# Cross-attention on one core: the score products of gU with ctxT_lo, on 64 rows and two heads at a time

## The chip, the core and the metric

The kernel runs on one core of a Trainium2 chip. The time is the device time of the whole program in microseconds (us). Before the change the median of 3 runs is 317.23 us (317.16 to 317.6).

## The reference

```python
Q = (img_embed @ Wq).reshape(B, -1, H, D).transpose(0, 2, 1, 3)
K = (sent_embed @ Wk).reshape(B, -1, H, D).transpose(0, 2, 1, 3)
V = (sent_embed @ Wv).reshape(B, -1, H, D).transpose(0, 2, 1, 3)
score = jnp.einsum('bhqd,bhkd->bhqk', Q, K) / math.sqrt(D)
mask = (atten_mask != 0)[:, None, None, :]
score = jnp.where(mask, score, -jnp.inf)
attn = jax.nn.softmax(score, axis=-1)
ctx = jnp.einsum('bhqk,bhkd->bqhd', attn, V).reshape(B, -1, H * D)
out = ctx @ Wo + img_embed
mu = jnp.mean(out, axis=-1, keepdims=True)
var = jnp.var(out, axis=-1, keepdims=True)
return (out - mu) * jax.lax.rsqrt(var + EPS) * gamma + beta
```

`img_embed` is x (8 x 256 x 256), `sent_embed` is ctx_768 (8 x 256 x 192): a batch of 8, 256 queries and 256 keys, 8 heads of size 256. All is float32.

## The kernel before

**What is multiplied.** The weights are folded first. A = Wq Wk^T of a head is 256 x 192, so a head's scores are (x A) ctx^T, and C = Wv Wo of a head is 192 x 256. The query side of a head, g = A^T x^T, has 192 rows: 128 lower ones (gL) and 64 upper ones (gU).

**Split operands.** A float32 operand is cut into a high part, rounded to the type fp32r, and the low part that is left; a product is then high x high, high x low and low x high, each a matmul in fp32r that adds into the same place of a PSUM bank. For the 64 upper rows one tile `gU` holds both parts of a head one above the other: for head 0 of a pair the high part stands on partitions 0 to 63 and the low part on 64 to 127, for head 1 the other way round. The host lays the upper 64 rows of ctx^T twice, so `ctxT_hi[:, 1]` and `ctxT_lo[:, 1]` carry them on both halves of the partitions. A matmul of `gU` with `ctxT_hi[:, 1]` on 128 rows therefore gives high x high and low x high at once. One with `ctxT_lo[:, 1]` gives high x low and, beside it, low x low, which the split does not need.

**Steps.** The work is 32 steps, one for each batch and pair of heads (`STEPS`, `PAIRS`). There is no scheduler: each engine's queue is written out by hand, with semaphores between the engines, and 24 of the steps stand in a loop over the batches. In one step TensorE (PE) does `scores(t)` (20 matmuls: 2 heads, 2 halves of the queries, 5 products), `query_products(t + 1)` (18 matmuls into gU_bank and gL_bank), `output_products(t - 4)` (18) and `context_products(t - 3)` (20 into tL_bank and tU_bank). The first four steps also have `fold_C`, which makes C: line 359 on whole tiles, line 365 with 64 columns of the stationary operand, so that its outputs are 64 partitions high. Line 365 is the only place where a matmul uses less than 128 rows and 128 columns of the array.

**Around the scores.** `gU` and `gL_hi` are written by ScalarE (ACT, line 576), the low parts by VectorE (DVE, line 745), one step ahead of their use. DVE reads the score banks (`maxima`, line 797): head 0 after the first count of `scores_done`, head 1 after the second. Then come the exponentials (ACT, line 619), the division by the sums (GpSimd, POOL, line 1021), and a transposition through a scratch in DRAM.

**scores (line 388).** For each head and each query half it issues five matmuls of 128 x 128 by 256 into one half of the head's bank: gU x ctxT_hi, gU x ctxT_lo, gL_hi x ctxT_hi, gL_hi x ctxT_lo and gL_lo x ctxT_hi. All go through `split_products` (line 320), so that the profile gives them line 325.

Of the kernel before, what the change touches and what calls it, by code (L numbers as in the profile page):

```python
# [13 lines left out]
P = 128  # L14
# [10 lines left out]
UP = DL - P  # L25
PAIRS = H // 2
STEPS = B * PAIRS
QT = S // P
# [15 lines left out]
def attention_kernel(nc, xT, x, ctxT, ctx, mask, wqT, wkT, wvT, wo, gamma, beta, out, scratch):  # L44
    es = ExitStack()
    with es:
        def sb(name, shape, dt=F32):
            return es.enter_context(nc.sbuf_tensor(name, shape, dt))

        def bank(name, shape):  # L50
            return es.enter_context(nc.psum_tensor(name, shape, F32))

        def sem(name):
            return es.enter_context(nc.semaphore(name))
# [20 lines left out]
        gL_hi = sb("gL_hi", [P, 2, S + APART], F32R)[:, :, 0:S]  # L75
        gL_lo = sb("gL_lo", [P, 2, S + APART], F32R)[:, :, 0:S]
        gU = sb("gU", [P, 2, S + APART], F32R)[:, :, 0:S]
# [4 lines left out]
        ctxT_hi = sb("ctxT_hi", [P, 2, KV], F32R)  # L82
        ctxT_lo = sb("ctxT_lo", [P, 2, KV], F32R)
# [37 lines left out]
        score_bank = [bank("score_bank0", [P, QT, KV]), bank("score_bank1", [P, QT, KV])]  # L121
# [57 lines left out]
        g_hi_done = sem("g_hi_done")  # L179
        g_split = sem("g_split")  # L180
        scores_done = sem("scores_done")
# [139 lines left out]
        def _(pe):  # L321
            def split_products(into, pairs, first=True, last=True, shared=False):

                for n, (stationary, moving) in enumerate(pairs):
                    ins = nc.tensor.matmul(into, stationary, moving, start=first and n == 0,  # L325
                                           stop=last and n == len(pairs) - 1, skip_group_check=shared)
                return ins
# [57 lines left out]
                tile(gL_bank[:, 0, :], col)  # L385
                tile(gL_bank[:, 1, :], col + P).then_inc(g_product, 1)

            def scores(t, j, b, heads=(0, 1)):

                if j == 0:  # L390

                    pe.wait_ge(ctxT_split, b + 1)
                for hh in heads:
                    if hh == 0:

                        pe.wait_ge(g_hi_done, 3 * t + 3)
                        pe.wait_ge(g_split, 3 * t + 2)
                    for q in range(QT):
                        rows = slice(q * P, (q + 1) * P)
                        hi, lo, up = gL_hi[:, hh, rows], gL_lo[:, hh, rows], gU[:, hh, rows]  # L400
                        split_products(score_bank[hh][:, q, :],
                                       [(up, ctxT_hi[:, 1, :]), (up, ctxT_lo[:, 1, :]),
                                        (hi, ctxT_hi[:, 0, :]), (hi, ctxT_lo[:, 0, :])], last=False)
                        if hh == 0 and q == 0:

                            pe.wait_ge(g_split, 3 * t + 3)
                        ins = split_products(score_bank[hh][:, q, :], [(lo, ctxT_hi[:, 0, :])], first=False)
                    ins.then_inc(scores_done, 1)

            def transposes(t):  # L410

# [107 lines left out]
            def step(t, j, b, folds=()):  # L519

                jb, bb = (j - LAG) % PAIRS, b - 1 if j < LAG else b
                ja, ba = (j + 1) % PAIRS, b + 1 if j == PAIRS - 1 else b
                scores(t, j, b)
                query_products(t + 1, ja, ba)
                if not (isinstance(t, int) and t < OUT_LAG):
                    output_products(t - OUT_LAG, j, b - 1)
                for pair in folds:
                    fold_C(pair)
                if not (isinstance(t, int) and t < LAG):
                    context_products(t - LAG, jb, bb)  # L530
# [15 lines left out]
            with pe.Fori(1, B - 1) as b:  # L546
# [3 lines left out]
                step(PAIRS * b + 5, 1, b + 1)  # L550
            step(STEPS - 2, 2, B - 1)
            scores(STEPS - 1, 3, B - 1)

            output_lowers(STEPS - 5, 3, B - 2)
# [587 lines left out]
```

## Time and profile before

| | |
|---|---|
| median of 3 runs | 317.23 us |
| profiled execution | 317.46 us |
| its span, first to last instruction | 315.7 us |
| PE busy | 308.8 us (98%) |
| PE's weight loads busy | 302.7 us (96%) |
| DVE, ACT, POOL busy | 253.1, 222.1, 181.4 us |
| mean granted TensorE clock | 0.997 |

PE is the row of the matmuls, PEld that of the weight loads, which run beside the matmuls. The matmuls are pipelined: a record lasts 0.28 us, while the next one starts about 0.11 us after it. So the time of a matmul in a dense stream is the distance from one start to the next. An fp32 matmul leaves two records, one in fp32r leaves one.

### The profile page before, as it was taken

The page shows a single profiled execution, that of the slowest core. Times are in us where ns is not written, and L with a number is a line of the kernel's source. Part 1 is how long each engine was busy: PE and PEld are TensorE (multiplying, and loading weights), DVE is VectorE, ACT ScalarE, POOL GpSimd, SP SyncE. Part 2 cuts the span into 40 slices and gives each one's busy share as a digit, 9 for nine tenths or more (in the row PEclk, how much of TensorE's full clock was granted, in tenths as well). Part 3 has the DMA queues.
Part 4 walks back from the last instruction along what each step waited for, and adds up shares of the span by engine and source line. Part 5 has one row for each costly group of instructions (what it writes and reads, how often), then busy time and mean ns, then how long its engine had stood idle before and what let it go on. Part 6 is the DMA issues. An engine that isn't in the chain of part 4 may idle for free.

```text
span 315.7 us, 8051 instructions
## 1 busy us (share of the span) xinstructions
PE 308.8 (98%) x2584; PEld 302.7 (96%) x2584; DVE 253.1 (80%) x721; ACT 222.1 (70%) x601; POOL 181.4 (57%) x183
## 2 busy tenths in 40 slices
PE   8999999999999999999999999999999999999993
PEld 7898889999999999999999999999999999999992
DVE  0467778777999879987998889987998889985686
ACT  2446678768867787678777797678767887777640
POOL 1123476457864587558855586458755686457212
PEclk9999999999999999999999999999999999999998
DMA  7995443464354553474445544364355535440101
GB/s 248 373 408 228 137 151 117 158 217 135 92 168 139 199 165 129 145 246 136 133 125 193 184 138 162 128 216 156 110 191 153 199 103 185 143 158 2 35 0 66
DMA packets 46912, 50.27 MB, mean 159 GB/s; under 512 B 3505, under 2 KB 37041, under 8 KB 46897
## 3 DMA queue, kind: packets, MB, share of 16 engines
q1 hardware_dynamic: 46608, 49.56, 46.7%
q10 hardware_dynamic: 288, 0.52, 0.7%
q8 instruction: 8, 0.13, 0.2%
q14 instruction: 8, 0.06, 0.1%
HBM read 32.24 MB, written 17.83 MB: 159 GB/s over the span
## 4 chain that ended last, share of the span: by engine, by line
PE 95%; DMA 2%; DVE 1%; SPq 1%; POOLq 0%; issue 0%; POOL 0%
PE score_bank L325 25%; PE out_bank L325 19%; PE gL_bank L325 14%; PE tL_bank L325 13%; PE tU_bank L325 9%; PE gU_bank L325 7%; DMA wq_raw<-in_wqT 2%; PE spare_bank L325 1%; PE spare_bank L359 1%; PE tL_bank L359 1%; PE tL_bank L341 1%; PE tU_bank L341 1%; PE tU_bank L365 1%; PE out_bank L365 1%; PE out_bank L341 0%; PE spare_bank L341 0%
## 5 line engine op out<-in xcount | busy, mean ns | idle before, releaser
L1021 POOL TENSOR_TENSOR probs<-probs,inv_sum 128x512 f32<-128x512 f32 x64 | 66.7, 1043 | 84.0 <-DVE inv_sum L808 83.4
L619 ACT ACTIVATE probs<-neg_scores,neg_max 128x256 f32<-128x256 f32 x128 | 64.2, 503 | 36.8 <-DVE neg_max L797 36.7
L1044 POOL TENSOR_TENSOR pT_lo<-pT_raw,pT_hi 128x512 fp32r<-128x512 f32 x60 | 76.7, 1298 | 8.6 <-ACT pT_hi L576 8.6
L797 DVE CUSTOM_DVE_ANT_0 neg_scores<-score_bank,mask_bias 128x256 f32<-128x256 f32 x128 | 49.2, 421 | 6.5 <-PE score_bank L325 4.0
L818 DVE STREAM_TRANSPOSE squares<-probs 128x512 f32<-128x512 f32 x60 | 42.4, 706 | 0.2
L576 ACT ACTIVATE tL_hi<-tL_bank 128x512 fp32r<-128x512 f32 x31 | 18.5, 598 | 28.4 <-PE tL_bank L325 28.4
L325 PE MATMUL score_bank<-ctxT_hi,gU 128*128 128x256 f32 x128 | 36.4, 284 | 0.0
L325 PE MATMUL score_bank<-ctxT_hi,gL_hi 128*128 128x256 f32 x128 | 36.0, 281 | 0.0
L325 PE MATMUL score_bank<-ctxT_lo,gU 128*128 128x256 f32 x128 | 35.9, 281 | 0.0
L325 PE MATMUL score_bank<-ctxT_hi,gL_lo 128*128 128x256 f32 x128 | 35.9, 280 | 0.0
L325 PE MATMUL score_bank<-ctxT_lo,gL_hi 128*128 128x256 f32 x128 | 35.8, 280 | 0.0
L325 PE MATMUL gL_bank<-xT_hi,A_lo 128*128 128x256 f32 x128 | 35.3, 276 | 0.0
L325 PE MATMUL gL_bank<-xT_lo,A_hi 128*128 128x256 f32 x128 | 35.3, 276 | 0.0
L325 PE MATMUL gL_bank<-xT_hi,A_hi 128*128 128x256 f32 x128 | 35.3, 276 | 0.0
L745 DVE TENSOR_TENSOR tL_lo<-tL_bank,tL_hi 128x512 fp32r<-128x512 f32 x31 | 21.4, 689 | 17.2 <-ACT tL_hi L576 17.1
L576 ACT ACTIVATE pT_hi<-pT_raw 128x512 fp32r<-128x512 f32 x60 | 34.3, 622 | 0.0
L325 PE MATMUL out_bank<-CL_lo,tL_hi 128*128 128x256 f32 x118 | 32.6, 276 | 0.0
L325 PE MATMUL out_bank<-CL_hi,tL_hi 128*128 128x256 f32 x118 | 32.6, 276 | 0.0
L325 PE MATMUL out_bank<-CL_hi,tL_lo 128*128 128x256 f32 x118 | 32.6, 276 | 0.0
L745 DVE TENSOR_TENSOR gU<-gU_bank,gU 64x256 fp32r<-64x256 f32 x64 | 27.1, 423 | 2.1
L845 DVE TENSOR_TENSOR tU<-tU_bank,tU_moved 64x256 f32<-64x256 f32 x62 | 26.0, 419 | 1.6 <-ACT tU_moved L660 0.6
L325 PEld LDWEIGHTS score_bank<-ctxT_hi,gU 128*128 128x128 f32 x128 | 24.0, 188 | 1.4 <-issue 1.2
(167 smaller groups left out, 980.6 us busy)
## 6 DMA issues: line engine op xcount, KB each, us to landing
scratch<-squares SPq DMA_DIRECT2D x30, 512.0 KB, 2.7
pT_raw<-scratch SPq DMA_DIRECT2D x120, 128.0 KB, 2.9
xT_raw<-in_xT SPq DMA_DIRECT2D x8, 256.0 KB, 4.4
ctxT_raw<-in_ctxT SPq DMA_DIRECT2D x8, 256.0 KB, 4.6
wo_raw<-in_wo SPq DMA_DIRECT2D x4, 512.0 KB, 13.7
x_res<-in_x SPq DMA_DIRECT2D x8, 256.0 KB, 3.0
out<-y_out SPq DMA_DIRECT2D x7, 256.0 KB, 2.5
wq_raw<-in_wqT SPq DMA_DIRECT2D x3, 512.0 KB, 7.6
```

The lines of the kernel that those rows point to most:

```text
L325: ins = nc.tensor.matmul(into, stationary, moving, start=first and n == 0, stop=last and n == len(pairs) - 1, skip_group_check=shared)
L341: ins = nc.tensor.matmul(dst[:, i * DL:(i + 1) * DL], wq_raw[:, h * DT + d, i * P:(i + 1) * P], wk_raw[:, h * DT + d, :], start=d == 0, st ...
L359: ins = nc.tensor.matmul(lower[:, hh, :], wv_raw[:, h * DT + d, 0:P], wo_raw[:, h * DT + d, :], start=d == 0, stop=d == DT - 1)
L365: ins = nc.tensor.matmul(upper[hh * UP:(hh + 1) * UP, 0, :], wv_raw[:, h * DT + d, P:DL], wo_raw[:, h * DT + d, :], start=d == 0, stop=d = ...
L576: return nc.scalar.activation(dst, src, ACT.Copy)
L619: nc.scalar.activation(probs[j % 2][:, n, :], neg_scores[:, n, :], ACT.Exp, bias=neg_max[:, n:n + 1], scale=-1.0, accum_out=row_sum[:, n:n ...
L745: return nc.vector.tensor_tensor(dst, whole, hi.bitcast(F32), ALU.subtract)
L797: nc.vector.tensor_tensor_reduce(out=neg_scores[:, n, :], in0=score_bank[hh][:, q, :], in1=mask_bias[:], scale=-SCALE, scalar=3.0e38, op0= ...
L818: nc.vector.transpose(squares[:, :, rows, :].rearrange("p s n c -> p n s c"), probs[j % 2][:, rows, :].rearrange("p n (s c) -> p n s c", c ...
L845: nc.vector.tensor_tensor(tU[part, :], places("tU", t)[0][part, hh, :], tU_moved[part, :], ALU.add).then_inc(tU_summed, 1)
L1021: nc.gpsimd.tensor_tensor(probs[j % 2][:, rows, :], probs[j % 2][:, rows, :], inv, ALU.mult) \
L1044: nc.gpsimd.tensor_tensor(pT_lo[j % 2][:, k].rearrange("p hh (q i r) -> p (hh q) i r", q=QT, i=ROWS), pT_raw[j % 2][:, k].rearrange("p i n ...
```

## The change

The product gU x ctxT_lo is computed on the 64 rows that hold the high part of a head alone: partitions 0 to 63 for head 0, 64 to 127 for head 1. The two heads' matmuls of a query half stand one behind the other (`pair_of_heads`), on different rows of the array and into different banks. One such pair stands ahead of query half 0 of head 0, and one ahead of query half 1 of head 0. The other four products of each head and half follow as before (`rest`). Since a pair writes both halves of both banks ahead of the rest, only the pair of query half 0 opens the accumulation of a bank. The waits at the head of a step stand for both heads; the wait for gL_lo stands ahead of the last product of head 0's first half, as before.

```diff
--- before.py
+++ after.py
@@ -385,27 +385,40 @@
                 tile(gL_bank[:, 0, :], col)
                 tile(gL_bank[:, 1, :], col + P).then_inc(g_product, 1)
 
-            def scores(t, j, b, heads=(0, 1)):
+            def scores(t, j, b):
 
                 if j == 0:
 
                     pe.wait_ge(ctxT_split, b + 1)
-                for hh in heads:
-                    if hh == 0:
-
-                        pe.wait_ge(g_hi_done, 3 * t + 3)
-                        pe.wait_ge(g_split, 3 * t + 2)
-                    for q in range(QT):
-                        rows = slice(q * P, (q + 1) * P)
-                        hi, lo, up = gL_hi[:, hh, rows], gL_lo[:, hh, rows], gU[:, hh, rows]
-                        split_products(score_bank[hh][:, q, :],
-                                       [(up, ctxT_hi[:, 1, :]), (up, ctxT_lo[:, 1, :]),
-                                        (hi, ctxT_hi[:, 0, :]), (hi, ctxT_lo[:, 0, :])], last=False)
-                        if hh == 0 and q == 0:
-
-                            pe.wait_ge(g_split, 3 * t + 3)
-                        ins = split_products(score_bank[hh][:, q, :], [(lo, ctxT_hi[:, 0, :])], first=False)
-                    ins.then_inc(scores_done, 1)
+                pe.wait_ge(g_hi_done, 3 * t + 3)
+                pe.wait_ge(g_split, 3 * t + 2)
+
+                def pair_of_heads(q):
+
+                    rows = slice(q * P, (q + 1) * P)
+                    for hh, part in enumerate((slice(0, UP), slice(UP, P))):
+                        split_products(score_bank[hh][:, q, :], [(gU[part, hh, rows], ctxT_lo[part, 1, :])],
+                                       first=q == 0, last=False, shared=True)
+
+                def rest(hh, q):
+
+                    rows = slice(q * P, (q + 1) * P)
+                    hi, lo, up = gL_hi[:, hh, rows], gL_lo[:, hh, rows], gU[:, hh, rows]
+                    split_products(score_bank[hh][:, q, :],
+                                   [(up, ctxT_hi[:, 1, :]), (hi, ctxT_hi[:, 0, :]), (hi, ctxT_lo[:, 0, :])],
+                                   first=False, last=False, shared=True)
+                    if hh == 0 and q == 0:
+
+                        pe.wait_ge(g_split, 3 * t + 3)
+                    return split_products(score_bank[hh][:, q, :], [(lo, ctxT_hi[:, 0, :])], first=False,
+                                          shared=True)
+
+                pair_of_heads(0)
+                rest(0, 0)
+                pair_of_heads(1)
+                rest(0, 1).then_inc(scores_done, 1)
+                rest(1, 0)
+                rest(1, 1).then_inc(scores_done, 1)
 
             def transposes(t):
```

The queue of PE in the second step, at head 0. A row is one matmul: bank written, moving operand, stationary operand, and the rows and columns of the output. Before:

```order
L325 MATMUL score_bank0<-ctxT_hi,gU 128x256
L325 MATMUL score_bank0<-ctxT_lo,gU 128x256
L325 MATMUL score_bank0<-ctxT_hi,gL_hi 128x256
L325 MATMUL score_bank0<-ctxT_lo,gL_hi 128x256
L325 MATMUL score_bank0<-ctxT_hi,gL_lo 128x256
L325 MATMUL score_bank0<-ctxT_hi,gU 128x256
L325 MATMUL score_bank0<-ctxT_lo,gU 128x256
L325 MATMUL score_bank0<-ctxT_hi,gL_hi 128x256
L325 MATMUL score_bank0<-ctxT_lo,gL_hi 128x256
L325 MATMUL score_bank0<-ctxT_hi,gL_lo 128x256
```

and at the same place now:

```order
L325 MATMUL score_bank0<-ctxT_lo,gU 128x256
L325 MATMUL score_bank1<-ctxT_lo,gU 128x256
L325 MATMUL score_bank0<-ctxT_hi,gU 128x256
L325 MATMUL score_bank0<-ctxT_hi,gL_hi 128x256
L325 MATMUL score_bank0<-ctxT_lo,gL_hi 128x256
L325 MATMUL score_bank0<-ctxT_hi,gL_lo 128x256
L325 MATMUL score_bank0<-ctxT_lo,gU 128x256
L325 MATMUL score_bank1<-ctxT_lo,gU 128x256
L325 MATMUL score_bank0<-ctxT_hi,gU 128x256
L325 MATMUL score_bank0<-ctxT_hi,gL_hi 128x256
L325 MATMUL score_bank0<-ctxT_lo,gL_hi 128x256
L325 MATMUL score_bank0<-ctxT_hi,gL_lo 128x256
```

The rows with ctxT_lo and gU are the ones on 64 rows, and each now has one of score_bank1 behind it; four matmuls on 128 rows stand between the two pairs. Behind that, at head 1, stood ten matmuls, and now eight:

```order
L325 MATMUL score_bank1<-ctxT_hi,gU 128x256
L325 MATMUL score_bank1<-ctxT_hi,gL_hi 128x256
L325 MATMUL score_bank1<-ctxT_lo,gL_hi 128x256
L325 MATMUL score_bank1<-ctxT_hi,gL_lo 128x256
L325 MATMUL score_bank1<-ctxT_hi,gU 128x256
L325 MATMUL score_bank1<-ctxT_hi,gL_hi 128x256
L325 MATMUL score_bank1<-ctxT_lo,gL_hi 128x256
L325 MATMUL score_bank1<-ctxT_hi,gL_lo 128x256
```

Head 1's two products with ctxT_lo and gU have gone from here to the pairs.

## Rows read from the trace of the kernel before

**Rows 1.** The page, busy times of the engines and their shares of the span

```profile
span 315.7 us, 8051 instructions
PE 308.8 (98%) x2584; PEld 302.7 (96%) x2584; DVE 253.1 (80%) x721; ACT 222.1 (70%) x601; POOL 181.4 (57%) x183
```

**Rows 2.** The page, the chain that ended last

```profile
PE 95%; DMA 2%; DVE 1%; SPq 1%; POOLq 0%; issue 0%; POOL 0%
```

**Rows 3.** Waits: who waited for whom, us in total, times, longest us

```profile
POOL probs L1021 <- DVE inv_sum L808: 83.4, 58, 4.4
ACT probs L619 <- DVE neg_max L797: 36.7, 56, 1.9
ACT tL_hi L576 <- PE tL_bank L325: 28.4, 30, 2.2
...
PE score_bank L534 <- POOL zeros L1006: 1.1, 1, 1.1
...
PE tL_bank L341 <- DMA wq_raw<-in_wqT: 0.5, 1, 0.5
```

**Rows 4.** Windows: busy us and count of each engine, clock, DMA share

```profile
50.00:304.00 254.00, 254.00 (x2219) 254.00 (x2218) 216.73 (x614) 191.81 (x516) 161.24 (x154) 1.00 0.45 146
```

**Rows 5.** Timeline of PE: start us, us, instruction; a step and the next

```profile
155.50 0.28 PE L325 MATMUL score_bank<-ctxT_hi,gU 128*128 128x256 f32 x1
155.62 0.28 PE L325 MATMUL score_bank<-ctxT_lo,gU 128*128 128x256 f32 x1
155.74 0.28 PE L325 MATMUL score_bank<-ctxT_hi,gL_hi 128*128 128x256 f32 x1
...
157.85 0.28 PE L325 MATMUL gU_bank<-xT_hi,A_hi 128*128 128x256 f32 x1
...
158.53 0.28 PE L325 MATMUL gL_bank<-xT_hi,A_hi 128*128 128x256 f32 x1
158.65 0.28 PE L325 MATMUL gL_bank<-xT_lo,A_hi 128*128 128x256 f32 x1
158.76 0.28 PE L325 MATMUL gL_bank<-xT_hi,A_lo 128*128 128x256 f32 x1
...
164.20 0.28 PE L325 MATMUL score_bank<-ctxT_hi,gU 128*128 128x256 f32 x1
```

**Rows 6.** Timeline of the weight loads at that step's start

```profile
155.50 0.19 PEld L325 LDWEIGHTS score_bank<-ctxT_lo,gU 128*128 128x128 f32 x1
155.62 0.19 PEld L325 LDWEIGHTS score_bank<-ctxT_hi,gL_hi 128*128 128x128 f32 x1
```

**Rows 7.** Timeline of PE around L365, from several windows

```profile
39.55 0.81 PE L359 MATMUL tL_bank<-wo_raw,wv_raw 128*128 128x256 f32 x3
39.98 0.38 PE L359 MATMUL tL_bank<-wo_raw,wv_raw 128*128 128x256 f32 x1
40.29 0.44 PE L365 MATMUL tU_bank<-wo_raw,wv_raw 128*64 128x256 f32 x2
40.55 0.61 PE L365 MATMUL tU_bank<-wo_raw,wv_raw 128*64 128x256 f32 x4
41.31 0.39 PE L325 MATMUL score_bank<-ctxT_hi,gU 128*128 128x256 f32 x1
41.53 0.28 PE L325 MATMUL score_bank<-ctxT_lo,gU 128*128 128x256 f32 x1
41.65 0.28 PE L325 MATMUL score_bank<-ctxT_hi,gL_hi 128*128 128x256 f32 x1
```

**Rows 8.** Timeline of the weight loads there, idle time before in brackets

```profile
40.28 0.15 PEld L365 LDWEIGHTS tU_bank<-wo_raw,wv_raw 128*64 128x64 f32 x2 [0.33 <-issue]
41.31 0.19 PEld L325 LDWEIGHTS score_bank<-ctxT_hi,gU 128*128 128x128 f32 x1 [0.39 <-issue]
41.41 0.19 PEld L325 LDWEIGHTS score_bank<-ctxT_lo,gU 128*128 128x128 f32 x1
```

**Rows 9.** Tiles tU_bank and score_bank: ns min/median/max, first and last start

```profile
L365 PEld LDWEIGHTS tU_bank<-wo_raw,wv_raw x16: 132/136/137, 33.0 to 40.8; 128*64 128x64 f32 x16
L365 PE MATMUL tU_bank<-wo_raw,wv_raw x16: 379/379/430, 33.0 to 41.0; 128*64 128x256 f32 x16
L325 PEld LDWEIGHTS score_bank<-ctxT_lo,gU x128: 187/188/192, 19.4 to 287.8; 128*128 128x128 f32 x128
```

**Rows 10.** Timeline of PE at its last step, behind a wait for DVE

```profile
308.03 0.39 PE L325 MATMUL spare_bank<-CL_hi,tL_hi 128*128 128x256 f32 x1
308.26 0.28 PE L325 MATMUL spare_bank<-CL_lo,tL_hi 128*128 128x256 f32 x1
```

**Rows 11.** Timeline of PE, from fp32r matmuls to fp32 ones

```profile
16.42 0.28 PE L325 MATMUL gL_bank<-xT_hi,A_lo 128*128 128x256 f32 x1
16.54 0.48 PE L341 MATMUL tL_bank<-wk_raw,wq_raw 128*128 128x192 f32 x2
```

**Rows 12.** Timeline of DVE around that step

```profile
153.75 0.69 DVE L745 TENSOR_TENSOR gL_lo<-gL_bank,gL_hi 128x512 fp32r<-128x512 f32 x1
159.49 0.42 DVE L797 CUSTOM_DVE_ANT_0 neg_scores<-score_bank,mask_bias 128x256 f32<-128x256 f32 x1
```

## Prediction

> **What bounds the kernel now.** I read the busy times first [rows 1]: PE has an instruction in flight for 308.8 of 315.7 us, and weight loads for 302.7 us; DVE follows with 253.1 us, ACT with 222.1, POOL with 181.4. The chain of work that ended last is PE for 95%, and a quarter of the span of it stands in score_bank [rows 2]. Then I asked who PE waits for [rows 3]: twice in the whole execution, 1.1 and 0.5 us, both before 10 us. In the loop it waits for nobody, and the clock is 1.00 between 50 and 304 us, which is the level of 2.4 GHz [rows 4]. So the kernel is a queue of matmuls on one engine. What is to be priced is how far apart two matmuls start, not how long one is drawn (0.28 us, since they are pipelined). In the timeline of a step [rows 5] the scores go from 155.50 to 157.85 us with 20 matmuls: 0.1175 us each. The gL_bank matmuls behind them start 0.113 apart. The step's loads start at the same distance, each just as the matmul ahead starts [rows 6]: a load is hidden behind the matmul ahead of it, and takes nearly as long. The next step starts at 164.20 us, 8.70 us later.
>
> **The change, part by part.** It touches PE alone. Each of the 32 steps had 20 score matmuls on 128 rows. It still has 20: 16 as before, and 4 on 64 rows, in two pairs. The two of a pair use different rows of the array and write different banks. So 32 x 2 = 64 pairs take the place of 128 full matmuls.
>
> *The gain by itself.* If the two of a pair run side by side, one slot of 0.118 us goes per pair. Side by side isn't seen for halves by rows before, but it is for halves by columns: L365 computes on 128 x 64 tiles, and its records come in twos [rows 7]. The first two take 0.44 us together where one takes 0.430 [rows 9], so the second starts some 0.013 us behind the first. The four from 40.55 on take 0.61 where one takes 0.379: the fourth starts 0.23 us behind the first, which is one more 0.013 and one step of 0.216 between the twos. (L359 has that step too, 0.215, but for single records: three take 0.81, one 0.379.) So a pair costs 0.118 + 0.013 = 0.131 in place of 2 x 0.1175 = 0.235 us: 0.104 us less, 64 x 0.104 = 6.7 us in all.
>
> *The switch.* The same place is the only one where PE changes from whole-array matmuls to part-array ones and back. Its cost can be read off as a whole. The last L359 matmul starts at 39.98 us, the second score matmul behind L365 at 41.53 us: 1.55 us. Between lie one L359 slot of 0.215 us (as above), four L365 steps of 0.216 and one score slot of 0.12: 1.20 us. The way in and out cost 0.355 us. The loads show what it is made of [rows 8]. The one of L365 isn't started with the matmul ahead, at 39.98, but at 40.28, and the first score load at 41.31, with no producer to wait for (both are put down to "issue"). The last two of L365 start at about 40.98 (40.55 and two steps) and would free the array at 41.20, so that load comes 0.11 late, and then stands in the open: second score matmul at 41.53, less a slot of 0.12, gives a true start at 41.41. That is 0.21 us out, hence 0.145 in. The way in is cheaper by its narrower load, 136 ns against 188 [rows 9]. The pairs of the change load 128 columns, so I put the way in at 0.145 + 0.052 = 0.197, the way out at 0.21: 0.41 us per visit.
>
> That an open load alone costs about half of that is seen where PE waited for DVE: load and matmul begin at 308.03, the next matmul 0.23 later, where 0.12 is usual [rows 10]. And it isn't the change between fp32 and fp32r operands: at 16.54 us fp32 matmuls of L341 follow fp32r ones of L325, all on whole tiles, at a plain 0.12 us [rows 11].
>
> The Trainium skill (TensorEngine Tiling (Array Packing), Key Properties) says that changing the tiling mode, and not just the tile, drains TensorE. The column halves agree with 0.355 us. By this rule row halves pay as well; what they pay no page says and no trace here shows.
>
> *Bounds of that unknown.* From below: halves by rows need no switch, and the pair's loads are hidden as all others are: 0 per visit. From above: a switch at 0.41 and the two loads or the two matmuls one behind the other, another 0.11: 0.52. I take 0.41 as the nearest row by kind, with the loads side by side as those of L365 are (two in 0.15 us, where one takes 0.136) [rows 8, 9].
>
> *The order of the work.* The kernel comes back to whole-array matmuls between the two pairs of a step, since half 0 of head 0 stands between: two visits a step, 64 in all, none shared. Every one is on the path, because PE waits for nobody.
>
> *Edits at nothing.* Bank 1 is written at the head of a step instead of ten matmuls later. Its readers, DVE's maxima of head 1, are through by 159.49 + 0.42 = 159.91 us, and the next step starts at 164.20 [rows 5, 12]. The wait for gL_lo stands ahead of the sixth score matmul instead of the fifth; it was written by 153.75 + 0.69 = 154.44 us, 1 us ahead of the step [rows 12]. Head 0 is complete after ten slots as before, head 1 after 18. Behind PE, ACT and POOL idle (POOL 83.4 us, ACT 36.7 and 28.4 [rows 3]); they neither lose by a slower PE nor hold up one that is 2% faster.
>
> *Sum.* Per pair 0.41 + 0.131 - 0.235 = +0.306 us; 64 x 0.306 = +19.6 us. The profiled execution took 317.46 us (a span of 315.7 and 1.8 around it), so 337.0 us. The median of the plain runs is 0.23 us below the profiled one: 336.8 us. Its own range is 333 (64 x 0.25, the visit at 0.355 us) to 338.
>
> **The rivals.**
> 1. *Row halves need no switch.* For it: all operands are fp32r, the outputs use all 128 partitions as before, only rows are left out, and L365 shows that parts of the array do run side by side. Against: nothing in the trace tells rows from columns, and columns pay. Price: -6.7 us, 310.5 us. This is the case on the other side; it decides below 0.104 us a visit. The Trainium skill (TensorE: Matmul & The Clock Gate, Part 3, The mechanism) speaks for it: loads are pulled ahead of running matmuls where the row groups differ, and matmuls of different tiles start about 4 ns apart. By its figure the gain would be an estimated 7.2 us, 310 us; L365 has 13 ns between its twos, by columns.
> 2. *No switch, but loads one at a time.* The change removes no load: 2584 loads before and after, each spaced 0.113 to 0.118 us. If loads of different rows can't overlap, the pair's two take two slots, and nothing is gained: 317.2 us. For it: the spacing is as much the loads' as the matmuls' [rows 6]. Against: L365's loads start 13 ns apart.
> 3. *Switch, and a pair one behind the other.* +0.306 + 0.11 = +0.41 us x 64 = +26.5 us: 343.7 us.
> 4. *A cheaper switch*, one way or without the open load: 0.15 to 0.3 a visit, +3 to +13 us: 320 to 330 us.
>
> **How the numbers follow.** A measurement of this kernel can tell about 0.2%, 0.6 us. Forecast 0.52; rival 1 0.22; rival 2 0.08; rival 3 0.12; rival 4 0.06. Slower: 0.52 + 0.12 + 0.06 = 0.70. Rival 2 lands within 0.2% for 0.06 and a little faster for 0.02; so faster 0.24, same 0.06. The range must reach from the forecast to rival 1, the larger of the others: 310 to 340 us, with rival 3 left out.
>
> **What would show it.** Right: the step's period grows from 8.70 to about 9.31 us; idle time of the weight loads ahead of `score_bank<-ctxT_lo,gU`, put down to issue, where it was 0.0; both score matmuls of a pair about 13 ns apart; the matmul behind a pair 0.3 us behind it; 2584 matmuls still. Wrong: a period of 8.49 us with the load of a pair standing beside the matmul ahead of it (rival 1), or 8.70 with loads of a pair 0.11 apart (rival 2), or a pair's matmuls over 0.1 us apart (rival 3).

## The result, and the profile after

The changed kernel takes 342.0 us (median of 4 runs, 341.87 to 342.15) against 317.33 us (4 runs) of the kernel before: a ratio of 1.0777, 95% interval 1.0758 to 1.0795. The forecast was 336.8 us with a range of 310 to 340. The direction is right, the time lies outside the range.

The page of the changed kernel, busy times. They answer to [rows 1]:

```profile
span 340.2 us, 8051 instructions
PE 332.4 (98%) x2584; PEld 309.6 (91%) x2584; DVE 254.3 (75%) x721; ACT 222.0 (65%) x601; POOL 180.8 (53%) x183
```

The span is 24.5 us longer, with the same number of matmuls. PE is as full as before, while the weight loads now have gaps. The wait list names no new wait of PE (its one wait for a weight transfer, before 10 us, is 1.4 us where it was 0.5 [rows 3], and its first L325 matmul starts at 14.32 us, before at 14.28); the other engines wait longer for it (POOL 108.8 us where it was 83.4 [rows 3]). So the time is in PE's own queue, at a clock of 1.00 as before (the windows below).

Two words are used from here on. A *slot* is the distance from one matmul's start to the next. A *visit* is PE going over to tiles of 64 rows and back to whole ones.

The start of a step in the timeline of PE (start us, us, instruction), to be read beside [rows 5]:

```profile
166.79 0.28 PE L325 MATMUL tU_bank<-pT_lo,ctxU 128*128 128x256 f32 x1
167.00 0.39 PE L325 MATMUL score_bank<-ctxT_lo,gU 64*128 64x256 f32 x2
167.31 0.39 PE L325 MATMUL score_bank<-ctxT_hi,gU 128*128 128x256 f32 x1
167.54 0.28 PE L325 MATMUL score_bank<-ctxT_hi,gL_hi 128*128 128x256 f32 x1
```

and the weight loads there:

```profile
166.68 0.19 PEld L325 LDWEIGHTS tU_bank<-pT_lo,ctxU 128*128 128x128 f32 x1
167.00 0.19 PEld L325 LDWEIGHTS score_bank<-ctxT_lo,gU 64*128 64x128 f32 x2
167.31 0.19 PEld L325 LDWEIGHTS score_bank<-ctxT_hi,gU 128*128 128x128 f32 x1
167.42 0.19 PEld L325 LDWEIGHTS score_bank<-ctxT_hi,gL_hi 128*128 128x128 f32 x1
```

This is the picture of L365 [rows 7, 8], now by rows. The two loads of a pair stand together, and so do its two matmuls: two in 0.39 us, where one takes 0.381:

```profile
L325 PE MATMUL score_bank<-ctxT_lo,gU x128: 380/381/383, 19.3 to 310.9; 64*128 64x256 f32 x128
```

They aren't started beside the matmul of 166.79 but 0.21 us behind it, and the load that follows comes at 167.31. From 166.79 to 167.54 pass 0.75 us, where four slots of 0.1175 (0.47) stood before: +0.28 us for a pair. 64 x 0.28 = 17.9 us.

That leaves 24.5 - 17.9 = 6.6 us. They are not at the pairs at all. (The visits of the first four steps are cheaper than the later ones; counted start by start over the whole trace, the visits take 17.6 us and the rest is 6.9.) The gL_bank matmuls, which the change doesn't touch, in the changed kernel:

```profile
170.90 0.28 PE L325 MATMUL gL_bank<-xT_hi,A_hi 128*128 128x256 f32 x1
171.02 0.28 PE L325 MATMUL gL_bank<-xT_lo,A_hi 128*128 128x256 f32 x1
171.14 0.28 PE L325 MATMUL gL_bank<-xT_hi,A_lo 128*128 128x256 f32 x1
171.25 0.28 PE L325 MATMUL gL_bank<-xT_hi,A_hi 128*128 128x256 f32 x1
```

They start 0.118 us apart, before 0.113 [rows 5]. The same holds for all 56 matmuls of a step that aren't scores. 56 x 0.0045 = 0.25 us a step, and with the two pairs (0.56) a step is 0.81 us longer. Windows, one row per kernel, from 60 to 280 us (busy us and count of each engine, granted clock, DMA share, GB/s), first the kernel before, then the changed one:

```profile
60.00:280.00 220.00, 220.00 (x1924) 220.00 (x1923) 191.79 (x548) 168.05 (x455) 143.56 (x137) 1.00 0.49 159
```

```profile
60.00:280.00 220.00, 220.00 (x1758) 207.65 (x1757) 174.75 (x496) 153.99 (x417) 132.46 (x126) 1.00 0.44 144
```

At 76 matmuls a step, 1924 are 8.69 us a step and 1758 are 9.51: 0.82 us longer, as the two parts give. The granted clock is 1.00 in both, its level of 2.4 GHz, so it has no part in this.

### The profile page after: what moved, and what is told of

It reads as the page before. It is cut to its first block, busy times and chain, and to the rows that moved or that the text cites. A ratio compares the mean times of both kernels' runs of the same rounds, so it can differ in the third digit from the quotient of the medians.

```text
span 340.2 us, 8051 instructions
## 1 busy us (share of the span) xinstructions
PE 332.4 (98%) x2584; PEld 309.6 (91%) x2584; DVE 254.3 (75%) x721; ACT 222.0 (65%) x601; POOL 180.8 (53%) x183
## 4 chain that ended last, share of the span: by engine, by line
PE 95%; DMA 2%; DVE 1%; SPq 0%; POOLq 0%; issue 0%; POOL 0%
PE score_bank L325 28%; PE out_bank L325 18%; PE gL_bank L325 13%; PE tL_bank L325 13%; PE tU_bank L325 9%; PE gU_bank L325 7%; DMA wq_raw<-in_wqT 2%; PE spare_bank L325 1%; PE tL_bank L359 1%; PE spare_bank L359 1%; PE tL_bank L341 1%; PE tU_bank L341 1%; PE out_bank L365 1%; PE tU_bank L365 1%; PE out_bank L341 0%; PE spare_bank L341 0%
## 5 line engine op out<-in xcount | busy, mean ns | idle before, releaser
L1034 POOL TENSOR_TENSOR probs<-probs,inv_sum 128x512 f32<-128x512 f32 x64 | 66.6, 1041 | 108.8 <-DVE inv_sum L821 108.8
L325 PE MATMUL score_bank<-ctxT_hi,gU 128*128 128x256 f32 x128 | 42.7, 334 | 0.0
L325 PE MATMUL score_bank<-ctxT_lo,gL_hi 128*128 128x256 f32 x128 | 36.3, 284 | 0.0
L325 PE MATMUL score_bank<-ctxT_hi,gL_hi 128*128 128x256 f32 x128 | 36.0, 282 | 0.0
L325 PE MATMUL score_bank<-ctxT_hi,gL_lo 128*128 128x256 f32 x128 | 36.0, 281 | 0.0
L325 PE MATMUL gL_bank<-xT_hi,A_lo 128*128 128x256 f32 x128 | 35.8, 280 | 0.0
L325 PE MATMUL gL_bank<-xT_hi,A_hi 128*128 128x256 f32 x128 | 35.7, 279 | 0.0
L325 PE MATMUL gL_bank<-xT_lo,A_hi 128*128 128x256 f32 x128 | 35.7, 279 | 0.0
L325 PE MATMUL out_bank<-CL_hi,tL_lo 128*128 128x256 f32 x118 | 33.0, 280 | 0.0
L325 PE MATMUL out_bank<-CL_lo,tL_hi 128*128 128x256 f32 x118 | 32.9, 279 | 0.0
L325 PE MATMUL out_bank<-CL_hi,tL_hi 128*128 128x256 f32 x118 | 32.9, 279 | 0.0
L325 PEld LDWEIGHTS score_bank<-ctxT_hi,gU 128*128 128x128 f32 x128 | 24.0, 187 | 8.2
L325 PE MATMUL tL_bank<-pT_hi,ctxL_hi 128*128 128x256 f32 x124 | 24.7, 280 | 0.0
```

The lines of the kernel that those rows point to most:

```text
L1034: nc.gpsimd.tensor_tensor(probs[j % 2][:, rows, :], probs[j % 2][:, rows, :], inv, ALU.mult) \
```

## The experiments

Below, the pace is the length of a slot among whole-tile matmuls: 0.113 us is the fast one, 0.118 the slow one. Three theories of the slow pace stand at the start. A: any restart of the stream of matmuls (a load that isn't hidden behind a matmul) sets it to 0.118 us, until something among the score matmuls brings back 0.113. B: only going over to part-array tiles does. C, later called O: the order of the score matmuls does. P came in after the first four runs: the places of the operands in SBUF have a part. In the edits `up`, `hi`, `lo` are gU, gL_hi and gL_lo.

**Order alone.** The pairs on all rows, at the changed kernel's places:

```diff
-                    for hh, part in enumerate((slice(0, UP), slice(UP, P))):
+                    for hh, part in enumerate((slice(0, P), slice(0, P))):
```

> The changed kernel's order of the score matmuls, but with gU x ctxT_lo on all 128 rows, as before the change. Theory A (going over to 64-row tiles and back costs about 0.39 us a visit, and each such restart also sets the stream of matmuls to a pace of 0.118 us in place of 0.113): no visit, no restart, so 317.3 us and 0.113 between gL_bank matmuls. Theory B (the switch itself, and nothing else that restarts PE, sets the slow pace): 317.3 us too. Theory C (the new order, two banks in turn and one start for a bank, sets the slow pace): 56 matmuls x 32 steps x 0.0045 us = 8 us more, 325 us.

Measured: 325.21 us (before 317.5; ratio 1.0236, 1.0219 to 1.0253). A and B miss it, C names it within 0.3 us. With no 64-row matmul in the kernel, gL_bank goes at 0.118:

```profile
153.47 0.28 PE L325 MATMUL gL_bank<-xT_hi,A_hi 128*128 128x256 f32 x1
153.59 0.28 PE L325 MATMUL gL_bank<-xT_lo,A_hi 128*128 128x256 f32 x1
153.71 0.28 PE L325 MATMUL gL_bank<-xT_hi,A_lo 128*128 128x256 f32 x1
```

The edit keeps three things of the new order together: the sequence of the products, the two banks in turn, and the single opening of a bank. No run separates them.

**Both pairs in front.**

```diff
                 pair_of_heads(0)
-                rest(0, 0)
                 pair_of_heads(1)
+                rest(0, 0)
```

> The changed kernel with both pairs at the head of the step, one behind the other: one visit a step in place of two. All theories: the visits fall from 64 to 32, and 32 x 0.39 = 12.5 us go: 329.5 us, if the pace stays at 0.118 us behind the scores. Theory A adds: 16 whole score matmuls now follow the restart without a second one (8 in the changed kernel), which is where the stream of the kernel before finds back to 0.113; if it does so here, another 7 to 8 us go: 322 us. Theory B: the pace stays slow, 329.5 us.

Measured: 329.12 us (1.0360, 1.0343 to 1.0377), with gL_bank at 0.118 still. That fits B and C, and not the quick recovery that A allowed. From the changed kernel it is 12.9 us down for 32 visits fewer, 0.40 us each. The one visit that is left, with its two pairs:

```profile
151.41 0.40 PE L325 MATMUL tU_bank<-pT_lo,ctxU 128*128 128x256 f32 x2
151.74 0.50 PE L325 MATMUL score_bank<-ctxT_lo,gU 64*128 64x256 f32 x4
152.17 0.39 PE L325 MATMUL score_bank<-ctxT_hi,gU 128*128 128x256 f32 x1
152.39 0.28 PE L325 MATMUL score_bank<-ctxT_hi,gL_hi 128*128 128x256 f32 x1
```

The second tU_bank matmul starts at 151.53 (0.40 for two, 0.28 for one). From there to 152.39 pass 0.86 us, where six slots of 0.118 (0.71) stood: +0.15 for a visit with two pairs against +0.28 with one. So a second pair in the same visit saves about 0.12 us.

**One 64-row matmul at the head of a step**, without a partner:

```diff
+                        part = slice(0, UP if hh == 0 and q == 0 else P)
                         split_products(score_bank[hh][:, q, :],
-                                       [(up, ctxT_hi[:, 1, :]), (up, ctxT_lo[:, 1, :]),
+                                       [(gU[part, hh, rows], ctxT_lo[part, 1, :]), (up, ctxT_hi[:, 1, :]),
```

> The kernel before with one matmul of each step, gU x ctxT_lo of head 0 and query half 0, on 64 rows and first in the step: one visit a step, with no partner beside it. Price of the visit alone: 32 x 0.39 = 12.5 us. Theory A: 19 whole score matmuls follow, the pace is back at 0.113 us before gL_bank: 330 us. Theory B: the switch leaves the pace at 0.118: 8 us more, 338 us.

Measured: 329.19 us (1.0365, 1.0348 to 1.0383): 11.7 us for 32 visits, 0.37 each, and no more. (In the loop alone a step takes 9.09 us where it took 8.70, 0.39 a visit; the first four are cheaper.) The timeline shows the passage, with the fourth group of score matmuls:

```profile
153.76 0.28 PE L325 MATMUL score_bank<-ctxT_hi,gL_lo 128*128 128x256 f32 x1
153.88 0.28 PE L325 MATMUL score_bank<-ctxT_lo,gU 128*128 128x256 f32 x1
153.99 0.28 PE L325 MATMUL score_bank<-ctxT_hi,gU 128*128 128x256 f32 x1
154.11 0.28 PE L325 MATMUL score_bank<-ctxT_hi,gL_hi 128*128 128x256 f32 x1
154.22 0.28 PE L325 MATMUL score_bank<-ctxT_lo,gL_hi 128*128 128x256 f32 x1
```

0.12 up to 153.88, 0.113 from there on, and so through the rest of the step. B, already missed by the first run, falls: this kernel goes over to a 64-row tile in every step, and the slow pace doesn't last.

**One 64-row matmul at the end of the scores:** gU x ctxT_lo moved to the end of each group of five, on 64 rows in the last.

> The kernel before with one matmul of each step, gU x ctxT_lo of head 1 and query half 1, on 64 rows and last among the step's scores: one visit a step. Theory A: the restart stands behind the score matmuls, nothing brings the pace back, the 56 others of a step go at 0.118 us: 317.3 + 12.5 + 8 = 338 us. Theory B: the same 338 us; if the place of the visit doesn't matter, this run and the one with the visit at the head are equal, under theory A this one is 8 us longer.

Measured: 337.80 us (1.0635, 1.0618 to 1.0653), as A and B both said. But the edit had moved the product in all four groups, and the pace was slow ahead of the visit too, so the order could explain it as well. The pair of runs with the last group alone, below, separates the two.

**A restart with no switch.** The kernel before, and behind the scores of each step:

```diff
+                pe.wait_ge(scores_done, 2 * t + 2)
```

> The kernel before, with one wait more in each step: behind its 20 score matmuls PE waits until the last of them is done (scores_done). All on whole tiles, order as before. Price of the wait itself, from a matmul's 0.28 us less its slot and an open load of 0.11: about 0.3 us, 32 x 0.3 = 9.6 us. Theory A (any restart of the stream sets the slow pace, 0.118 us, until score matmuls bring the fast one back): the 56 others of a step are slow, 8 us more, 335 us. Theory B (only going over to part-array tiles does it): 327 us. Theory O (the order of the score matmuls alone decides the pace, restarts don't): 327 us.

Measured: 334.76 us (two runs, 333.86 and 335.66; 1.0538, 1.0469 to 1.0606). The time is A's (the two runs are 0.5% apart); its parts are another matter. A step whose pace is slow behind the wait:

```profile
165.44 0.28 PE L325 MATMUL score_bank<-ctxT_lo,gL_hi 128*128 128x256 f32 x1
165.55 0.28 PE L325 MATMUL score_bank<-ctxT_hi,gL_lo 128*128 128x256 f32 x1
165.89 0.39 PE L325 MATMUL gU_bank<-xT_hi,A_hi 128*128 128x256 f32 x1
166.11 0.28 PE L325 MATMUL gU_bank<-xT_lo,A_hi 128*128 128x256 f32 x1
166.23 0.28 PE L325 MATMUL gU_bank<-xT_hi,A_lo 128*128 128x256 f32 x1
166.35 0.28 PE L325 MATMUL gU_bank<-xT_hi,A_hi 128*128 128x256 f32 x1
...
```

It was 0.113 up to 165.55 and is 0.118 from 166.11 on, on whole tiles throughout. But the step ahead of it, in the same trace, stays fast:

```profile
156.45 0.28 PE L325 MATMUL score_bank<-ctxT_hi,gL_lo 128*128 128x256 f32 x1
156.86 0.38 PE L325 MATMUL gU_bank<-xT_hi,A_hi 128*128 128x256 f32 x1
157.08 0.28 PE L325 MATMUL gU_bank<-xT_lo,A_hi 128*128 128x256 f32 x1
157.19 0.28 PE L325 MATMUL gU_bank<-xT_hi,A_lo 128*128 128x256 f32 x1
157.31 0.28 PE L325 MATMUL gU_bank<-xT_hi,A_hi 128*128 128x256 f32 x1
```

Of 26 restarts between 50 and 290 us, 20 left the slow pace and 6 the fast one, every fourth. It isn't chance. The 20 are alike (the next matmul starts 0.334 us behind the last score matmul), and so are the 6 (0.410 us), and the 6 are always the same step of a batch, that of the fourth pair of heads. There `query_products` goes on to the next batch: it reads the first columns of A, and PE has a further wait, for xT_split, right behind the added one. The fourth step ahead of the loop goes over to the same operands behind the same further wait (at 45.01 us), but starts after 0.334 us, and its gL_bank matmuls go at 0.118. So the operands alone don't make it fast; what goes with the pace in all of these restarts is how late the next matmul starts. So A needs a softer form: a restart can set either pace, and mostly sets the slow one. The wait itself was about as dear as expected: 165.55 to 166.11 is 0.56 us where two slots (0.23) stood, 0.33 us; 156.45 to 157.08 gives 0.40.

**The last group alone, on 64 and on 128 rows.** The first three groups as in the kernel before; in the fourth gU x ctxT_lo comes last, once on 64 rows and once on 128. The cut below is shortened, and `FROM` stands for `UP` in the first kernel and for `0` in the second:

```diff
+                        late = hh == 1 and q == 1
...
+                                             [(lo, ctxT_hi[:, 0, :])] + ([(gU[FROM:, hh, rows], ctxT_lo[FROM:, 1, :])] if late else []),
```

> The kernel before, with only the step's last group of five changed: for head 1 and query half 1, gU x ctxT_lo comes last and on 64 rows (the first 15 score matmuls of a step stay as they were). One visit a step, behind the scores. Theories A and B: fast pace at the group before, lost by the visit: 317.3 + 12.5 + 8 = 338 us. Theory O: if the same order on 128 rows keeps the fast pace, so does this one: 330 us.

> The same order as the kernel with the 64-row matmul last, but on 128 rows: no visit. Theories A and B: 317.3 us, as the first 15 score matmuls have brought the fast pace by then. Theory O: 317.3 us if the order of the first three groups decides, 325 us if that of the last.

Measured: 337.64 us on 64 rows (1.0628, 1.0598 to 1.0659), 317.55 us on 128 (1.0000, 0.9989 to 1.0011). This is the clean pair: one order, and going over to 64 rows costs 20.1 us. The 64-row kernel at the visit:

```profile
158.01 0.28 PE L325 MATMUL score_bank<-ctxT_lo,gL_hi 128*128 128x256 f32 x1
158.13 0.28 PE L325 MATMUL score_bank<-ctxT_hi,gL_lo 128*128 128x256 f32 x1
158.33 0.38 PE L325 MATMUL score_bank<-ctxT_lo,gU 64*128 64x256 f32 x1
158.64 0.39 PE L325 MATMUL gU_bank<-xT_hi,A_hi 128*128 128x256 f32 x1
158.87 0.28 PE L325 MATMUL gU_bank<-xT_lo,A_hi 128*128 128x256 f32 x1
158.99 0.28 PE L325 MATMUL gU_bank<-xT_hi,A_lo 128*128 128x256 f32 x1
159.11 0.28 PE L325 MATMUL gU_bank<-xT_hi,A_hi 128*128 128x256 f32 x1
```

0.113 ahead of it, 0.118 behind. From 158.13 to 158.87 pass 0.74 us where three slots of 0.113 (0.34) stood: 0.40 for the visit, 12.8 us for 32. The rest, 7.3 us, is the pace. O as the only cause falls.

**Placement.** The order of the first experiment, on 128 rows, and one number changed:

```diff
-STREAM_LEAD = 32
+STREAM_LEAD = 64
```

> The changed kernel's order on 128 rows (325.2 us), with the filler tile ahead of xT_hi 64 in place of 32 elements wide, so that all moving operands behind it stand 128 bytes further in each partition against gU, gL and A. Same instructions in the same order. Theory P (slots differ in length because the weight load and the moving operand meet in SBUF, so the pace hangs on where they stand): the time changes by several us, and slots with another length are seen. Theory O (order alone): 325 us and the same slots.

Measured: 317.19 us (ratio to the kernel before 0.9984, 0.9972 to 0.9995), where the same instructions took 325.21. 128 bytes more between the stationary operands' tiles and the moving ones' decide 8 us. (Every tile behind the filler moves by them, those of the other engines too.) The fast pace sets in with the fourth group of scores:

```profile
156.81 0.28 PE L325 MATMUL score_bank<-ctxT_hi,gL_lo 128*128 128x256 f32 x1
156.93 0.28 PE L325 MATMUL score_bank<-ctxT_hi,gU 128*128 128x256 f32 x1
157.04 0.28 PE L325 MATMUL score_bank<-ctxT_hi,gL_hi 128*128 128x256 f32 x1
157.15 0.28 PE L325 MATMUL score_bank<-ctxT_lo,gL_hi 128*128 128x256 f32 x1
157.27 0.28 PE L325 MATMUL score_bank<-ctxT_hi,gL_lo 128*128 128x256 f32 x1
157.38 0.28 PE L325 MATMUL gU_bank<-xT_hi,A_hi 128*128 128x256 f32 x1
```

**The changed kernel at that placement**, the same one-line edit:

> The changed kernel itself (64-row pairs, two visits a step), with the filler tile 64 elements wide in place of 32. If restart and placement decide the pace together, this is the visits' price alone, as far as the last score matmuls bring back the fast pace: 64 x 0.277 = 17.7 us, 335.2 us. If the second visit comes too late in the step for that (eight whole score matmuls behind it), 342 us as before.

Measured: 333.87 us (1.0512, 1.0494 to 1.0529): 8.1 us less than the changed kernel, and 16.2 above the one before, 0.253 for a pair. The pace is back within the eight score matmuls behind the second visit:

```profile
155.94 0.28 PE L325 MATMUL score_bank<-ctxT_lo,gL_hi 128*128 128x256 f32 x1
156.05 0.28 PE L325 MATMUL score_bank<-ctxT_hi,gL_lo 128*128 128x256 f32 x1
156.18 0.28 PE L325 MATMUL score_bank<-ctxT_hi,gU 128*128 128x256 f32 x1
156.29 0.28 PE L325 MATMUL score_bank<-ctxT_hi,gL_hi 128*128 128x256 f32 x1
156.40 0.28 PE L325 MATMUL score_bank<-ctxT_lo,gL_hi 128*128 128x256 f32 x1
```

The time is 1.3 us under the expectation mostly because the first four steps cost less: their scores are 0.27 to 0.33 us longer than in the kernel before, where a step of the loop is 0.52 or 0.55 us longer.

**Both pairs in front, at that placement:**

> Both pairs at the head of the step (one visit, 329.1 us at the slow pace), with the filler tile 64 wide. 16 whole score matmuls follow the visit: the pace should come back, 56 x 32 x 0.0045 = 8 us less, 321 to 322 us, still above the kernel before. If the pace doesn't hang on the placement here, 329 us.

Measured: 320.99 us (1.0112, 1.0095 to 1.0128), as expected; 8.1 us below the same order with the filler 32 wide. One visit with two pairs costs 3.3 us in all; each pair still doesn't earn its half of a visit.

**The kernel before at two other placements**, `STREAM_LEAD` 64 and 128:

> The kernel before with the filler tile 64 wide, nothing else. Its 56 other matmuls of a step are at 0.113 us already, so only the 20 score matmuls (0.1175) can change: between 314.5 us (all at 0.113) and 317.3 us; if this order doesn't find the fast pace at this placement, 325 us.

> The kernel before with the filler tile 128 wide. Placement theory: another distance between the loads' and the moving operands' places gives other slots, so the time moves by up to 3 us down or 8 us up. Order alone: 317.3 us.

Measured: 318.03 us for both (1.0013 and 1.0014, each 1.0004 to 1.0023). The order of the kernel before finds the fast pace at all three placements tried, and the hoped-for faster scores didn't come. The fastest kernel here is the new order on 128 rows with the wider filler, 0.16% under the kernel before. That is within what the prediction counted as no change, though its interval excludes 1.

## Why the prediction missed

**Where PE's cost stands: right.** The kernel is PE's queue, nothing else came to bind.

**The switch: right, in kind and size.** Row halves pay, and about what the prediction took from the column halves and the wider load: it put a visit at 0.41 us. In the changed kernel the pair's load starts at 167.00, where the array was free at 166.91 (166.79 and a slot): 0.09, and then 0.11 for the open load. The next load starts 0.31 behind it, which is that load, the pair's own 0.11 and 0.09 more; it is open for another 0.11 (167.31 to 167.42). So 0.09 + 0.11 + 0.09 + 0.11 = 0.40 us a visit; the step from two visits to one gives 0.40 as well. The rule of the Trainium skill (TensorEngine Tiling (Array Packing), Key Properties) that a change of the tiling mode drains TensorE holds for row tiles here, with 0.39 to 0.40 us a visit in the loop. Rivals 1, 2 and 4 are out.

**The pair: right, a little better.** The two records start 0.004 us apart (0.39 for two, 0.381 for one), not 0.013, which makes a pair 0.009 us cheaper. What is measured is the sum of visit and pair; split by the rows above, a pair takes 0.11 in place of 0.131. The 0.004 us are also what the Trainium skill gives for tiles of different rows (TensorE: Matmul & The Clock Gate, Part 3, The mechanism: about 4 ns). Rival 3, one behind the other, is out, though its 343.7 us came nearest to the 342.0 measured: that is coincidence. With both terms the pair comes to +0.28 instead of +0.306, 1.7 us less than forecast.

**What failed is a term that the sum put at nothing: what the change does to the 56 matmuls of a step that it doesn't touch.** "It touches PE alone" was followed by a price for the pairs only, and "Edits at nothing" put the new order at nothing. Both took the 0.113 us between the other matmuls as fixed. It is a state. The same gL_bank matmuls go at 0.113 or 0.118, and what stands ahead of them is part of what decides. The new order alone costs 7.7 us at this placement (325.21 against 317.5), which none of the rivals held. In the changed kernel the term is 6.6 us by the difference above. The pace is the same in both kernels, 0.25 us a step in each of the 27 steps of 56 such matmuls, 6.7 us; the profiled run with the order alone also started its first L325 matmul 0.5 us later than the kernel before (14.80 and 14.28 us). 19.6 - 1.7 + 6.6 = 24.5 us, the difference of the spans. Without the pace the forecast would have held: at the other placement the changed kernel took 333.87 us, inside the prediction's own range of 333 to 338. The new order alone is enough for the slow pace in those 27 steps. That the visits have a part too is seen in the second to fourth steps, which stand behind L365: the gL_bank matmuls there go at 0.113 us in the changed kernel and at 0.118 with the order alone.

**The profile before had shown it.** In [rows 11] gL_bank is followed after 0.12 us, and I called that "plain"; in [rows 10] the same distance was called "usual". In the loop it was 0.113 for gL_bank [rows 5]. Two paces for one instruction form stood in the rows, and these slow ones stood in the start-up and right behind a wait, at 308.03. But a slow pace with neither stood in the loop itself, in every step, where the prediction read only its mean (0.1175):

```profile
157.28 0.28 PE L325 MATMUL score_bank<-ctxT_hi,gU 128*128 128x256 f32 x1
```

This is the first matmul of the fourth group of scores. From the step's start at 155.50 to here are 15 slots of 0.119 us, from here to the next step at 164.20 [rows 5] 61 of 0.113. So the kernel before loses the fast pace with the first score matmul of every step, without a wait or a visit, and finds it again in the fourth group. The slow pace doesn't need a restart. At this placement the new order keeps the fast one from coming back; a visit or most restarts behind the scores take it away again. The range could have held 342 us from these alone: 56 x 32 x 0.0045 = 8 us on top of 336.8 at most.

**What stays open.** Shown: an order, a placement, a visit or a restart each change the pace, with times. Not shown: by what. That loads and moving operands meet in SBUF is argued from the one fact that 128 bytes between them decide it in the three kernels tried with the new order (8 us each) and not in the kernel before; no row shows a conflict. Nor is it known why the first score matmul loses the fast pace, which property of the old order brings it back in the fourth group, or why the restart that comes 0.08 us later was harmless.

## What to carry to other kernels

Price a part-array matmul in a stream of whole ones by the visit, not by the slot it saves: here 0.40 us against 0.12 saved by a pair. An estimate from the two is that it takes more than three pairs in one visit to win; no run here had more than two. In a kernel that is one dense queue of matmuls, read the slots of the same line at several places first, over ten matmuls or more, since 5 ns do not show in one; if there are two values, what lies ahead is a state, and any new order, wait or tile can tip it for every matmul behind. When a kernel's time moves by more than the edited instructions can account for, shift the operands' places by a filler tile and run it again before the edit is blamed.

## What the hardware showed that was not expected

- One and the same stream of 128 x 128 by 256 matmuls in fp32r runs at 0.113 or 0.118 us a matmul at a clock of 1.00, and holds either for some fifty matmuls. 4% of PE's time hang on it.
- 128 bytes of filler between the stationary and the moving operands moved one order of instructions from 325.21 to 317.19 us, and hardly moved another (317.66 and 318.03 us).
- A wait of PE for its own last matmul, on whole tiles, costs 0.33 us in 20 of 26 steps and 0.40 in 6, about as much as the visit to a 64-row tile. The 20 leave the slow pace behind them, the 6 the fast one.
- Two 64-row matmuls on different rows start 0.004 us apart, and so do their weight loads of 128 columns.
